# Attention of a fused cross-attention and mixture-of-experts kernel: the two best logits handled once per four pairs, reciprocals and logits moved in PSUM, rows stored four steps later

## The reference

```python
# x, ctx: (64, 128, 256) fp32 = 64 sequences ("batches") of 128 rows of 256 values
h = layernorm(x)                                   # over the 256 values of a row
score = softmax(einsum('bci,bcj->bij', ctx, h) / 16, axis=0)   # axis 0 is the batch
x = x + einsum('bci,bij->bcj', ctx, score)
t = layernorm(x).reshape(8192, 256)
logits = t @ router_w.T                            # 8 experts
l, idx = top_k(logits, 2); p = softmax(l)
y = sum over the two chosen e of p[e] * (gelu(t @ w1[e].T + b1[e]) @ w2[e].T + b2[e])
out = x + y
```

## Time and profile before

| | |
|---|---|
| median of the runs | 858.28 us |
| profiled execution, first to last instruction | 909.8 us |
| stage 3, VectorE's first L832 to its last L818 | 156.4 to 292.4 us |
| TensorE busy | 770.1 us (85%) |
| VectorE busy | 622.8 us (68%) |
| ScalarE busy | 390.1 us (43%) |
| GpSimd busy | 574.0 us (63%) |

### The profile page before, as it was taken

How to read it: one execution, slowest core, us unless ns; L and a number is a source line. 1 busy time by engine, 2 the same in 40 slices (tenths; PEclk the granted TensorE clock), 3 DMA queues, 4 the chain that set the end, 5 groups by cost and what they waited for, 6 DMA issues and landing times. The chain is left out here.

```text
span 909.8 us, 22499 instructions
## 1 busy us (share of the span) xinstructions
PE 770.1 (85%) x5931; PEld 649.5 (71%) x5932; DVE 622.8 (68%) x1520; ACT 390.1 (43%) x715; POOL 574.0 (63%) x815
## 2 busy tenths in 40 slices
PE   6999996999996449888989887989588889879886
PEld 5678885878885338766877776978367778767775
DVE  6998999899998758655655654363465656556554
ACT  3555664576666204333333433143133333334331
POOL 5664776788884056666576566366766666665663
PEclk9999997999997559999999999799789999999998
DMA  7887773488885124444344443343533343333330
GB/s 227 251 250 240 237 228 114 137 269 266 267 275 192 53 60 134 131 147 157 118 148 156 142 133 119 112 140 76 159 106 111 106 129 108 97 115 116 96 107 2
DMA packets 82200, 137.20 MB, mean 151 GB/s; under 512 B 10075, under 2 KB 55140, under 8 KB 82032
## 3 DMA queue, kind: packets, MB, share of 16 engines
q0 software_dynamic: 23104, 68.43, 24.9%
q1 hardware_dynamic: 59056, 68.26, 23.9%
HBM read 94.56 MB, written 47.59 MB: 156 GB/s over the span
## 5 line engine op out<-in xcount | busy, mean ns | idle before, releaser
L680 PE MATMUL psum<-work,w1T_high 128*128 128x256 f16 x1248 | 227.4, 285 | 53.5 <-ACT work L1067 36.6
L1059 ACT ACTIVATE work<-psum,slots 128x256 f32<-128x256 f32 x312 | 130.2, 471 | 309.4 <-PE psum L680 233.0
L703 PE MATMUL psum<-w2T_high,slots 128*128 x1248 | 214.7, 277 | 6.2 <-issue 5.1
L680 PEld LDWEIGHTS psum<-work,w1T_high 128*128 x1248 | 124.0, 102 | 85.9 <-issue 67.2
L680 PE MATMUL psum<-work,w1T_low 128*128 128x256 f16 x624 | 177.6, 285 | 3.5 <-issue 3.5
L703 PE MATMUL psum<-w2T_low,slots 128*128 x624 | 172.4, 276 | 1.7 <-issue 1.7
L952 DVE CAST slots<-work 128x512 f16<-128x512 f32 x156 | 71.0, 455 | 138.4 <-ACT work L1059 114.8
L703 PEld LDWEIGHTS psum<-w2T_high,slots 128*128 128x128 f16 x1248 | 119.6, 99 | 23.2 <-issue 9.2
L561 PE MATMUL psum<-slots,work 128*128 (+1 forms) x512 | 124.0, 392 | 7.4 <-ACT slots L991 6.8
L540 POOL DMA_INDIRECT rows_second<-slots x78 | 82.3, 1055 | 66.0 <-issue 35.6
L968 DVE SCALAR_TENSOR_TENSOR slots<-psum,slots 128x256 f32<-128x256 f32 x156 | 68.2, 478 | 78.5 <-remote 63.9
(11 more groups left out here) (126 smaller groups left out, 1125.2 us busy)
## 6 DMA issues: line engine op xcount, KB each, us to landing
work<-in_ctx SPq DMA_DIRECT2D x96, 256.0 KB, 3.5
rows_first<-slots SPq DMA_DIRECT2D x32, 514.0 KB, 3.9
slots<-in_x SPq DMA_DIRECT2D x32, 256.0 KB, 3.8
work<-in_L_ffn_w SPq DMA_DIRECT2D x32, 256.0 KB, 3.2
work<-in_x SPq DMA_DIRECT2D x32, 256.0 KB, 3.1
slots<-rows_first,slots POOLq DMA_INDIRECT x86
rows_second<-slots POOLq DMA_INDIRECT x78
slots<-rows_second,slots POOLq DMA_INDIRECT x78
```

Source lines behind the costliest of these rows:

```text
L680: mm = pe.matmul(h, w1T[pw][:, f, c, bass.ds(e * P, P)], xT[r2][:, (px * HC + c) * GROUP:(px * HC + c + 1) * GROUP], start=(c == 0 and px ...
L703: mm = pe.matmul(y, act16[r2][pa][:, f * GROUP + s * P:f * GROUP + (s + 1) * P], w2T[pw][:, f, bass.ds(e * DIM, DIM)], start=(f == 0 and p ...
L1059: last = act.activation(act32[r2][:, f * GROUP:(f + 1) * GROUP], psum[:, 2 + 2 * r2 + f // 2, (f % 2) * GROUP:(f % 2 + 1) * GROUP], ACT.Ge ...
```

## The change

The small operations on the two best logits (`gap`, exp, `den`, `p1`, `p2`, the copy to `choice`) are done once for four pairs, on 8 or 16 values per partition instead of 2 or 4, when the fourth pair of a block has come to them. `top` and `topi` get four slots. exp moves from lag 6 to 7, the probabilities from 7 to 8, the store from 8 to 12, and its wait becomes one for the block. The reciprocals of VectorE's 192 columns go to bank 6 of PSUM and are read from there. The logits of all pairs go to bank 7, so the matmul of a pair waits for `max_index` of the pair just before it.

```diff
+        share = psum[:, 6, 0:2 * DIM - PROD_POOL]
+        logits = psum[:, 7, 0:16]
...
-        L_CT, L_PV, L_XN, L_LOWX, L_XNT, L_LG, L_P = 1, 2, 4, 5, 5, 6, 7
-        L_XL, L_STORE = 1, 8
+        L_CT, L_PV, L_XN, L_LOWX, L_XNT, L_LG, L_EXP, L_P = 1, 2, 4, 5, 5, 6, 7, 8
+        L_XL, L_STORE = 1, 12
+
+        def closes(i, k, lag):
...
+            return live(i, k, lag, PAIRS) and (k - lag) % RING == RING - 1
...
-                    sp.wait_ge(a_p2, m + 1)
+                    sp.wait_ge(a_p2, block_of_it)
...
                     pe.wait_ge(a_xnTs, m + 1)
-                    after(pe, a_topi, m - 1)
+                    after(pe, a_topi, m)
...
-            dve.reciprocal(ssum[:, PROD_POOL:], ssum[:, PROD_POOL:]).then_inc(e_recip, 1)
+            dve.wait_ge(e_wlow, PAIRS // 2)
+            dve.reciprocal(share, ssum[:, PROD_POOL:]).then_inc(e_recip, 1)
...
-                    dve.tensor_tensor(gap[:, r2, :], top[:, r2, :, 1], top[:, r2, :, 0], ALU.subtract).then_inc(a_gap, 1)
-                    for j in range(2):
-                        last = dve.max_index(topi[:, r2, j, :], top[:, r2, j, :], psum[:, 6 + r2, j * 8:j * 8 + 8])
+                    if closes(i, k, L_LG):
+                        tops = top[:].rearrange("p q j w -> p (q j) w")
+                        dve.tensor_tensor(gap[:], tops[:, :, 1], tops[:, :, 0], ALU.subtract).then_inc(a_gap, 1)
+                    for j in range(2):
+                        last = dve.max_index(topi[:, r4, j, :], top[:, r4, j, :], logits[:, j * 8:j * 8 + 8])
...
-                if live(i, k, L_P, PAIRS):
-                    m, r2 = i + k - L_P, (k - L_P) % 2
-                    dve.wait_ge(a_p1, m + 1)
...
+                if closes(i, k, L_P):
+                    wait_apart(dve, a_p1, n + (k - L_P) // RING + 1)
+                    dve.tensor_tensor(probs(n, k, L_P, 1), probs(n, k, L_P, 0), egap[:], ALU.mult).then_inc(a_p2, 1)
...
-            dve.wait_ge(a_choice, PAIRS)
+            dve.wait_ge(a_choice, PAIRS // RING)
```

More of the change, by code:

```diff
@@ L186, in xattn_ffn @@
         shift = sb("shift", [P, RING, 2])
-        top = sb("top", [P, 2, 2, 8])
-        topi = sb("topi", [P, 2, 2, 8], U32)
+        top = sb("top", [P, RING, 2, 8])
+        topi = sb("topi", [P, RING, 2, 8], U32)
         warm = sb("warm", [P, 1])
-        gap = sb("gap", [P, 2, 2])
-        egap = sb("egap", [P, 2, 2])
-        den = sb("den", [P, 2, 2])
+        gap = sb("gap", [P, 2 * RING])
+        egap = sb("egap", [P, 2 * RING])
+        den = sb("den", [P, 2 * RING])
         psum = stack.enter_context(nc.psum_tensor("psum", [P, 8, 512], F32))
+        share = psum[:, 6, 0:2 * DIM - PROD_POOL]
+        logits = psum[:, 7, 0:16]
         def slot(b, first, n):
@@ L617, in attend @@
                 if live(i, k, L_LG, PAIRS):
-                    m, r = i + k - L_LG, (k - L_LG) % 2
+                    m = i + k - L_LG
                     pe.wait_ge(a_xnTs, m + 1)
-                    after(pe, a_topi, m - 1)
+                    after(pe, a_topi, m)
                     for j in range(2):
                         for h in range(HC):
-                            mm = pe.matmul(psum[:, 6 + r, j * 8:j * 8 + 8], a_xnT[:, j, h * P:(h + 1) * P], rwT[:, h, :], start=(h == 0), stop=(h == HC - 1))
+                            mm = pe.matmul(logits[:, j * 8:j * 8 + 8], a_xnT[:, j, h * P:(h + 1) * P], rwT[:, h, :], start=(h == 0), stop=(h == HC - 1))
                     mm.then_inc(a_logit, 1)
@@ L782, in attend @@
                     dve.tensor_tensor(slot2(m * 2, XN + P, P).bitcast(F16), a_xnr[:, 2 * r:2 * r + 2, :], slot2(m * 2, XN, P).bitcast(F16), ALU.subtract).then_inc(a_low, 1)
-                if live(i, k, L_P, PAIRS):
-                    m, r2 = i + k - L_P, (k - L_P) % 2
-                    dve.wait_ge(a_egap, m + 1)
-                    dve.tensor_scalar(den[:, r2, :], egap[:, r2, :], WSCALE, WSCALE, ALU.mult, ALU.add).then_inc(a_den, 1)
+                if closes(i, k, L_P):
+                    wait_apart(dve, a_egap, n + (k - L_P) // RING + 1)
+                    dve.tensor_scalar(den[:], egap[:], WSCALE, WSCALE, ALU.mult, ALU.add).then_inc(a_den, 1)
                 if live(i, k, L_LG, PAIRS):
-                    m, r2 = i + k - L_LG, (k - L_LG) % 2
+                    m, r4 = i + k - L_LG, (k - L_LG) % RING
                     wait_apart(dve, a_logit, m + 1)
                     for j in range(2):
-                        last = dve.max(top[:, r2, j, :], psum[:, 6 + r2, j * 8:j * 8 + 8])
+                        last = dve.max(top[:, r4, j, :], logits[:, j * 8:j * 8 + 8])
                     last.then_inc(a_top, 1)
@@ L832, in attend @@
                     dve.tensor_tensor(slot2(m * 2, PROD_POOL, 2 * DIM - PROD_POOL), slot2(m * 2, PROD_POOL, 2 * DIM - PROD_POOL),
-                                      ssum[:, PROD_POOL:].unsqueeze(1).to_broadcast([P, 2, 2 * DIM - PROD_POOL]), ALU.mult).then_inc(a_probv, 1)
+                                      share.unsqueeze(1).to_broadcast([P, 2, 2 * DIM - PROD_POOL]), ALU.mult).then_inc(a_probv, 1)
             pipeline(dve, PAIRS, RING, 2 * RING, L_P, attend)
@@ L1033, in attend @@
                     act.activation(slot2(m * 2, XN, P).bitcast(F16), a_xnr[:, 2 * r:2 * r + 2, :], ACT.Copy).then_inc(a_high, 1)
[L1034 to L1038, removed]
+                if closes(i, k, L_EXP):
+                    act.wait_ge(a_gap, n + (k - L_EXP) // RING + 1)
+                    act.activation(egap[:], gap[:], ACT.Exp).then_inc(a_egap, 1)
+            pipeline(act, PAIRS, RING, 2 * RING, L_EXP, attend)
             for r in range(RING):
```

26 lines of the change are left out of this document (13 added, 13 removed).

## The result

The changed kernel takes 872.65 us (median of 4 runs, 867.07 to 877.64), the kernel before 857.81 us in the same series (855.77 to 863.21). The ratio is 1.0161 with a 95% interval of 1.0106 to 1.0216, so the change costs 13.8 us (9.1 to 18.5). Forecast were +6.5 us and 864.8 us. The sign is right, the size is half of what came, and 872.65 lies just above the range that ended at 871.

The account below looks back on a forecast made before the run. The prediction took a VectorE-GpSimd cycle of 3.85 us a step (3.90 in the trace) to bound the attention. Its terms, 6.1 - 0.6 + 0 + 1.0 = +6.5 us on 858.3, gave 864.8 us; range 853 to 871.

Parts of the forecast that it names:

- which ring closes: Attention loop: logits wait for max_index, which waits through L797 for the product queued behind the logits; 3.91 us a step.
- the ring doesn't close: Rival: TensorE's own pace of 3.55 us decides the attention steps, giving 849.9 us, faster; chance 0.12.
- I take 0.04: Attention step: hand-overs from max_index to logits and from product to L797, 0.04 us each.
- `gap` held: Attention loop: VectorE's merged gap waits for GpSimd's L490 to end, 0.87 us once in four steps; bounds 0 and 1.43.
- The 0.07 for the reciprocal of eight values: Attention loop: this VectorE reciprocal lies in the TensorE-VectorE cycle in another step of each block, adding 0.07 us.
- between 0 and -1.3, taken 0: Ahead of TensorE's step 8: possible gain from reading VectorE's reciprocals in PSUM.
- -0.6: End of attention: L797 of step 33 starts at once instead of 0.62 us behind L633's end.
- The +1: End of attention: L851 1.5 us earlier without GpSimd's iota, or +3.2 if the iota comes first; taken between them.
- `gap` is not held, or the old ring: Rival: gap is through before L490, or VectorE and GpSimd still set 3.90 us a step; about 859 us, chance 0.25.
- `p2` meets L490 as well: Rival: p2 in a block's last step also waits for L490, +8.6 at most; likely 869.1 us, slower; chance 0.13.
- 6.1: Attention loop, TensorE's steps 8 to 33: 25 steps at 0.245 us extra each, from blocks of 16.58 against 15.60 us.

Follow-up runs that it names:

- run 1: Changed kernel with logits in two banks again, the max_index wait one pair looser, and reciprocals back in SBUF: 854.46 us, 0.9955 of the kernel before.
- run 6: Changed kernel with the attention product moved ahead of the logits on TensorE, one bank kept: 851.27 us, 0.9905 of the kernel before.
- run 3: Changed kernel with gap moved behind max_index: 865.77 us, 1.0065 of the kernel before.
- run 4: Kernel before with only the logits put in one bank and the wait for max_index of the pair just before: 891.65 us, 1.0389.
- Run 2: Changed kernel with only VectorE's reciprocals back in SBUF: 873.67 us, 1.0174 of the kernel before.
- run 5: Kernel before with logits in one bank, the tighter max_index wait, and gap behind max_index: 874.50 us, 1.0198.
- Run 7: Kernel before with only the attention product moved ahead of the logits on TensorE: 859.86 us, 1.0011.
- run 8: Changed kernel with the attention product ahead of the logits, two logits banks, and reciprocals in SBUF: 853.59 us, 0.9959 of the kernel before.
- run 9: Changed kernel with the attention product ahead of the logits and gap behind max_index: 848.63 us, 0.9889 of the kernel before.

## Why the prediction was right in kind and wrong in size

**Right: which ring closes.** L637 waits for `max_index` in nearly every step, L811 for L647, and runs 1 and 6 open the ring by its two ends (the wait, and what is queued behind it): 854.5 and 851.3 us. The rival "the ring doesn't close" falls. Its price was 849.9, which is about what the kernel gives when the ring is opened by hand.

**Wrong: the step "I take 0.04" for the two hand-overs.** This is the term of the sum that failed. The hand-over from `max_index` to the logits had no row and took 0.14 us. That from the product to L797 (now L811) took 0.26 us behind the modelled end of a 1.98 us matmul; the 0.03 us of the forecast was a single place in step 3, behind one of 2.66 us. The Trainium skill (Perfetto Trace Analysis, Tensor Engine Instruction (MATMUL, LD_WEIGHTS)) says that TensorE's end in a profile is "a model, not a measurement", so this interval would be the model's error and the hand-over together. The trace agrees so far that the same hand-over shows as 0.03 us in one place and as 0.26 in another. The two together are 0.40 us instead of 0.08, which alone takes a bare step from 3.91 to 4.23 us; the trace has 4.19 to 4.26, on average 4.22: 25 x 0.31 = +7.8 us. The forecast named both hand-overs but gave them no upper end, and so the range ended too low.

**Nearly right: `gap` held.** Forecast +0.87 us per block, found 4.94 - 4.22 = 0.72 us by the steps and 0.78 us by run 3. It was held as worked out from L490's place, for 0.86 us. The 0.07 for the reciprocal of eight values doesn't show: the step that holds it (L814 at 248.99) takes 4.20 us, no more than its neighbours. The forecast's 25 steps have 6.25 blocks with 0.94 us each for these two terms, 5.9 us; the trace has six holds of 0.72, 4.3 us: 1.6 too high.

**Not thought of: the clock.** 0.94 us here, in one step. The forecast had TensorE wait in every step and did not ask what idle time does to its clock. It is small here, and large in run 4.

**Start and end.** Taken 0 and found +1.0 us ahead of step 8. Run 2 tells two parts of it apart: from the first product (step 2) to that of step 8 it takes 180.31 - 157.73 = 22.6 us, the changed kernel 179.09 - 157.41 = 21.7, the kernel before 178.09 - 157.22 = 20.9. So the ring, in which L637 waits for 1.08 us already at 174.18, costs about 1.7 us there, and the reciprocals in PSUM give back 0.9, which the forecast had as "between 0 and -1.3, taken 0". Taken -0.6 + 1.0 and found -1.1 at the end. The +1 stood for "the iota holds L851"; the iota came first, by 0.14 us, and didn't hold it (below).

**The rivals.** "`gap` is not held, or the old ring" falls: 0.86 us, and L845 at 0.555 and L832 at 0.157 us are free. "`p2` meets L490 as well", 869.1 us, was nearest in time but falls too: L832's maximum is 0.174 us in the changed kernel. Its closeness is chance.

**The sum.** Two small terms remain: the last of the 25 steps takes 4.03 us, 0.2 less than the others, and the kernel before took 97.8 us for its 25 where the forecast counted 97.5. So 6.1 should have been 6.1 + 7.8 - 1.6 + 0.9 - 0.2 - 0.3 = 12.7; the trace has 12.8. With +1.0 and -1.1 it is 12.7, the runs have 13.8 (9.1 to 18.5).

## What to carry to other kernels

When two users of a buffer become one, write down the ring that the new wait closes and how many steps it spans. A ring of one step has every hand-over in it, and each of these must be priced from rows of the same two engines with instructions of the same length, with an upper end, because the error counts once per step. Then ask what is queued behind the waiting instruction: moving the product ahead of the logits turned a loss of 1.6% into a gain of 1.0% with the same buffers and the same work. A tiny instruction with two SBUF inputs can stand for nearly a whole GpSimd instruction (up to 1.38 us beside one of 1.43, in run 5), so its place (in the ring or behind the signal that the ring waits for) matters more than its work.

## What the runs showed of the hardware that was not expected

**The iota holds some instructions and not others.** In the changed kernel L864 ran its usual 1.23 us beside it. Run 7 has all kinds in one place (GpSimd, then VectorE):

```profile
287.90 4.67 POOL L498 IOTA slots<- 128x4992 f16 x1 [3.99 <-DMA rows_first<-slots]
```

```profile
288.25 0.16 DVE L805 TENSOR_TENSOR gap<-top 128x2 f32<-128x2 f32 x1
...
288.62 0.14 DVE L818 TENSOR_TENSOR slots<-slots,egap 128x2 f32<-128x2 f32 x1
288.74 3.86 DVE L823 CAST smax<-topi 128x4 f32<-128x4 uint32 x1
288.82 3.79 DVE L786 TENSOR_SCALAR den<-egap 128x2 f32<-128x2 f32 x1
```

The copy and `den` stand until the iota's end (287.90 + 4.67 = 292.57, against 292.60 and 292.61), as `den` did before. The two products with two SBUF inputs, L805 and L818, run free, though the same L818 is held by L490 in the loop. The Trainium skill (SBUF — State Buffer, Who interferes with whom) has the distinction that the forecast lacked: an operation with two SBUF inputs contends with a GpSimd instruction that reads SBUF, "not with one that only writes it", while copies and `tensor_scalar` in a two-port mode contend with GpSimd without that exception. The iota has no input, L490 and L504 have two; these rows agree. In which mode L823 and L786 ran, the trace doesn't show.

**The same read from PSUM is not held.** L845 has a maximum of 0.558 us in run 6, L843 of run 8 with the same work from SBUF one of 1.779 us, each in part beside GpSimd's long product.

**The clock falls after short idle times.** One pause of 1.20 us stood ahead of the only fall in the loop of the changed kernel; but the same pause at 258.76 had none behind it: the step that follows has its 1.98 us product. The ring isn't needed for a fall: runs 1, 6, 7 and 9 have one each, behind waits for context of 1.72, 1.88, 1.89 and 1.28 us. Runs 3 and 8, whose longest pauses in the loop are 0.53 and 1.07 us, have none. In run 4, with pauses of 1.23 and 1.25 us, the mean over ten us was 0.83 in many windows, and yet a pause of 1.54 us (ahead of 185.05) had no fall behind it. What decides isn't shown by these runs.
